# Graph attention network on one core: operands of VectorE's long instructions moved from SBUF to PSUM, and a new order of scores, messages and transposes

## What is computed

```
m = xl[src] + xr[dst]
e = einsum('ehd,hd->eh', leaky_relu(m, 0.2), att)
emax = segment_max(e, dst);  ex = exp(e - emax[dst])
denom = segment_sum(ex, dst);  alpha = ex / denom[dst]
out = segment_sum(alpha[..., None] * xl[src], dst)
```

## Time and profile before

| | us |
|---|---|
| median of 3 runs (lowest to highest) | 7290.55 (7282.23 to 7300.37) |
| span of the profiled execution | 7290.4 |
| busy in it: PE / DVE / ACT / POOL | 4733.5 / 4893.6 / 4079.6 / 5179.0 |
| share of the span: PE / DVE / ACT / POOL | 65% / 67% / 56% / 71% |
| mean granted clock of TensorE | 0.792 |

### The profile page before, as it was taken

The page is one execution under the profiler, slowest core; times in us unless marked ns, Lnnn a source line. Parts: engine busy times, 40 slices in busy tenths (PEclk is TensorE's granted clock), DMA queues, the critical chain, the costliest instruction groups (busy, mean ns, idle before and its releaser), DMA issues. The chain is left out here.

```text
span 7290.4 us, 132506 instructions
## 1 busy us (share of the span) xinstructions
PE 4733.5 (65%) x30647; PEld 4262.1 (58%) x30647; DVE 4893.6 (67%) x9144; ACT 4079.6 (56%) x9739; POOL 5179.0 (71%) x5105
## 2 busy tenths in 40 slices
PE   2777776577777567777746666645666654666663
PEld 2677775466767457777635565535555553555553
DVE  5777886467777557777655555546777765777776
ACT  1555554466766457667623333326767654767672
POOL 4777774377777577777657777757777766777774
PEclk6777787788888778888868778867888876888886
DMA  2677775289998578898847777735555553555553
GB/s 71 183 192 194 194 196 157 69 251 258 259 261 256 154 219 258 255 261 255 228 116 208 206 203 206 206 102 148 159 159 159 159 139 97 159 159 159 159 159 88
DMA packets 1717674, 1334.47 MB, mean 183 GB/s; under 512 B 384948, under 2 KB 1559891, under 8 KB 1717524
## 3 DMA queue, kind: packets, MB, share of 16 engines
q1 hardware_dynamic: 1516788, 837.31, 40.0%
q0 software_dynamic: 200736, 495.45, 24.8%
HBM read 913.26 MB, written 418.79 MB: 183 GB/s over the span
## 5 line engine op out<-in xcount | busy, mean ns | idle before, releaser
L739 POOL DMA_INDIRECT s_rows<-kv_tab,s_idx x2352 | 2359.8, 1003 | 737.3 <-issue 703.8
L739 POOL DMA_INDIRECT s_rows<-xl_tab,s_idx x1568 | 1622.5, 1035 | 491.6 <-issue 476.8
L902 PE MATMUL bank<-s_qwin,s_hot_t 128*128 128x128 f32 (+1 forms) x9408 | 1657.2, 342 | 12.9 <-ACT s_hot_t L766 7.1
L928 PE MATMUL bank<-s_msg,s_hot 128*128 128x144 f32 (+1 forms) x9408 | 1553.5, 313 | 126.1 <-ACT s_part L810 90.9
L902 PEld LDWEIGHTS bank<-s_qwin,s_hot_t 128*128 128x128 f32 x9408 | 1557.9, 256 | 57.0 <-issue 31.0
L928 PEld LDWEIGHTS bank<-s_msg,s_hot 128*128 128x128 f32 x9408 | 1351.1, 211 | 189.0 <-ACT s_part L810 145.1
L917 PE MATMUL bank<-ident,s_alpha 128*32 128x128 f32 (+1 forms) x588 | 182.6, 310 | 1512.8 <-DVE s_alpha L1042 1506.1
L810 ACT ACTIVATE s_part<-bank 128x288 f32<-128x288 f32 (+1 forms) x2352 | 901.2, 403 | 352.5 <-PE bank L928 299.7
L917 PEld LDWEIGHTS bank<-ident,s_alpha 128*32 128x32 f32 (+1 forms) x588 | 62.6, 107 | 1598.6 <-issue 1598.4
L780 ACT ACTIVATE s_gap<-iota_free,rank_col 128x128 bf16<-128x128 f32 x3136 | 989.5, 387 | 0.1
L798 ACT ACTIVATE s_prob<-s_diff 32x128 f32<-32x128 f32 (+1 forms) x588 | 180.3, 307 | 1436.2 <-DVE s_diff L997 1407.5
(11 more groups left out here) (292 smaller groups left out, 6193.9 us busy)
## 6 DMA issues: line engine op xcount, KB each, us to landing
s_qwin<-q_tab SPq DMA_DIRECT2D x3920, 64.0 KB
part_tab<-s_part SPq DMA_DIRECT2D x294, 576.0 KB
part_tab<-s_part SPq DMA_DIRECT2D x294, 544.0 KB
s_attr_t<-attr_tab SPq DMA_DIRECT2D x196, 512.0 KB
attr_tab<-s_attr_t SPq DMA_DIRECT2D x98, 512.0 KB
s_rows<-kv_tab,s_idx POOLq DMA_INDIRECT x2352
s_rows<-xl_tab,s_idx POOLq DMA_INDIRECT x1568
s_attr<-in_edge_attr SPq DMA_DIRECT2D x97, 256.0 KB
```

What stands on the lines that cost most here:

```text
L739: pool.indirect_dma_start(out=rows[u][:, t, :], out_offset=None, in_=tab, in_offset=bass.IndirectOffsetOnAxis(ap=idx[u][:, t:t + 1], axis= ...
L902: ins = pe.matmul(q_ps[h][:, (t - h * per) * QW:(t - h * per + 1) * QW], hot_t[:, t, :], qwin[u][:, t, :], start=True, stop=True)
L928: ins = pe.matmul(part_ps[c % 2][:, t * W:(t + 1) * W], hot[u][:, PAIR * c + t, :], msg[:, PAIR * c + t, :], start=True, stop=True)
```

## The change

In `edge_sweep`:

- Constants (the row 0..127 for the one-hots, Wt, bt, att) are copied once a sweep from SBUF into PSUM bank 4, and the one-hots, the angles and the product with att read them there. The angle itself is kept in bank 2, and the first scan's result `fwd` in bank 5.
- messages read probabilities and maxima from PSUM. `copy_probs` and `pm` are gone; `msg` has two buffers; turn_alpha(i) waits for messages(i-1) in place of copy_probs(i-1).
- gatv2: the add (new L1036) writes into the q bank in place, ScalarE `slopes` (new L805) multiplies the bank by 0.2 into `prod`, and VectorE `weigh` takes the maximum of bank and `prod` (new L1048), multiplies with att (new L1050) and sums (new L1051). Both adds stand before both weighs.
- gat: the one-hots are bf16 too and ScalarE casts them; the last step of the angles, -|a|, becomes `folds` on ScalarE (Abs) with a negative scale in the cosine; angles stand before the scores; turn_attr and copy_attr go half by half through one bank.
- In every sweep messages(n-1) stay behind all of scores(n) on VectorE.

```diff
-        hot_ps = [pl.banks[0], pl.banks[2]] if kind == "gat" else [pl.banks[0][:, :].bitcast(BF16)]
+        hot_ps = pl.banks[0][:, :].bitcast(BF16)
         q_ps = [pl.banks[1], pl.banks[2]]
         e_ps = [pl.banks[3], pl.banks[4]]
+        if kind == "gat":
+            ang_ps, turn_ps = pl.banks[2], pl.banks[3]
+        const = pl.banks[4]
+        iota_ps, Wt_ps, bt_ps, att_ps = const[:, 0:P], const[:, P:P + 64], const[:, P + 64:2 * P], const[:, P:2 * P]
         small = pl.banks[5]
         alpha_t = small[0:R, 0:P]
+        fwd = small[0:R, 3 * P:4 * P]
         prob_ps, max_ps = small[:, P:P + R], small[:, P + R:P + 2 * R]
         part_ps = [pl.banks[6], pl.banks[7]]
 
...
-                def copy_probs(i, k, u, n):
-                    wait(act, prob_turned, i + 1)
-                    if n >= 1:
-                        wait(act, msg_done, 3 * i)
-                    act.activation(pm[:, :], small[:, P:P + 2 * R], ACT.Copy).then_inc(prob_copied, 1)
+                def slopes(i, k, u, n):
+                    for h in range(2):
+                        wait(act, added, 2 * i + h + 1)
+                        act.activation(prod[h][:, :, :].rearrange("p t d -> p (t d)"), q_ps[h][:, :], ACT.Copy, scale=0.2
+                                       ).then_inc(slope_done, 1)
...
+                def folds(i, k, u, n):
+                    wait(act, angle_done, i + 1)
+                    act.activation(ang2[u][:, :, :], ang2[u][:, :, :], ACT.Abs).then_inc(folded, 1)
...
                     if has(n, 1):
                         copy_hot(*near(*g, 1))
+                    if kind == "gatv2" and has(n):
+                        slopes(*g)
                     if has(n, -2):
                         copy_parts(*near(*g, -2), 0)
                         copy_parts(*near(*g, -2), 1)
-                    if has(n, -1):
-                        copy_probs(*near(*g, -1))
...
                 def turn_alpha(i, k, u, n):
                     wait(pe, alpha_done, QB * (i + 1))
                     if n >= 1:
-                        wait(pe, prob_copied, i)
+                        wait(pe, msg_done, 3 * i)
                     settle(pe, pe_passed)
                     pe.transpose(alpha_t, alpha[:, :, :].rearrange("p t h -> p (t h)"), pl.ident[:, :]
                                  ).then_inc(alpha_turned, 1)
...
-                    out = hot[u] if kind == "gat" else hot_b[u % 2]
-                    v.tensor_tensor(out[:, :, :], bc(pl.iota_free[:, :].unsqueeze(1), [P, G, P]),
+                    v.tensor_tensor(hot_b[u % 2][:, :, :], bc(iota_ps.unsqueeze(1), [P, G, P]),
                                     bc(pl.rank_col[:, bass.ds(i * G, G)].unsqueeze(2), [P, G, P]),
                                     ALU.is_equal).then_inc(hot_built, 1)
...
+                def scores(i, k, u, n, h):
+                    if h == 0:
+                        wait(v, gathered[u], 16 * G * (k + 1))
+                        if n >= 1:
+                            wait(v, alpha_turned, i)
+                    wait(v, q_done, 2 * i + h + 1)
+                    t0, t1 = h * HALF, (h + 1) * HALF
+                    q = q_ps[h][:, :].rearrange("p (t d) -> p t d", t=HALF)
+                    if kind == "tconv":
+                        e = e_ps[h][:, :].rearrange("p (t d) -> p t d", t=HALF)
+                        kv = rows[u][:, t0:t1, :].rearrange("p t (a d) -> p t a d", a=2)
+                        v.tensor_tensor(kv, kv, bc(e.unsqueeze(2), [P, HALF, 2, D]), ALU.add).then_inc(e_used, 1)
+                        wait(v, e_used, 2 * i + h + 1)
+                    if kind == "gatv2":
+                        v.tensor_tensor(q, q, rows[u][:, t0:t1, :], ALU.add).then_inc(added, 1)
+                    else:
+                        v.tensor_tensor(prod[h][:, :, :], q, rows[u][:, t0:t1, 0:D], ALU.mult).then_inc(q_used, 1)
+                        wait(v, q_used, 2 * i + h + 1)
                         v.tensor_reduce(alpha[:, t0:t1, :], prod[h][:, :, :].rearrange("p t (h c) -> p t h c", c=C),
                                         AX.X, ALU.add).then_inc(alpha_done, 1)
 
+                def weigh(i, k, u, n, h):
+                    then = stepper(i, h)
+                    wait(v, slope_done, 2 * i + h + 1)
+                    t0, t1 = h * HALF, (h + 1) * HALF
+                    flat = prod[h][:, :, :].rearrange("p t d -> p (t d)")
+                    v.tensor_tensor(flat, q_ps[h][:, :], flat, ALU.max).then_inc(q_used, 1)
+                    wait(v, q_used, 2 * i + h + 1)
+                    then(v.tensor_tensor(prod[h][:, :, :], prod[h][:, :, :], bc(att_ps.unsqueeze(1), [P, HALF, D]), ALU.mult))
+                    v.tensor_reduce(alpha[:, t0:t1, :], prod[h][:, :, :].rearrange("p t (h c) -> p t h c", c=C),
+                                    AX.X, ALU.add).then_inc(alpha_done, 1)
+
                 def angles(i, k, u, n):
 
 
+                    wait(v, gathered[u], 16 * G * (k + 1))
                     then = stepper(i)
                     fl = "p t c -> p (t c)"
-                    a, tn = ang[:, :, :].rearrange(fl), turns[:, :, :].rearrange(fl)
+                    a, tn = ang_ps[:, :], turns[:, :, :].rearrange(fl)
+                    a3 = a.rearrange("p (t c) -> p t c", t=G)
                     then(v.tensor_tensor(rel[:, :], rows[u][:, :, D + H], pl.weight_col[:, bass.ds(i * G, G)], ALU.subtract))
                     then(v.tensor_tensor(ang[:, :, :], bc(rel[:, :].unsqueeze(2), [P, G, 64]),
-                                         bc(w["Wt"][:, :].unsqueeze(1), [P, G, 64]), ALU.mult))
-                    then(v.tensor_tensor(ang[:, :, :], ang[:, :, :], bc(w["bt"][:, :].unsqueeze(1), [P, G, 64]), ALU.add))
+                                         bc(Wt_ps.unsqueeze(1), [P, G, 64]), ALU.mult))
+                    then(v.tensor_tensor(a3, ang[:, :, :], bc(bt_ps.unsqueeze(1), [P, G, 64]), ALU.add))
                     then(v.tensor_scalar(tn, a, float(1 / (2 * np.pi)), MAGIC, ALU.mult, ALU.add))
                     then(v.tensor_scalar(tn, tn, MAGIC, None, ALU.subtract))
                     then(v.scalar_tensor_tensor(a, tn, -TWO_PI_HIGH, a, ALU.mult, ALU.add))
-                    then(v.scalar_tensor_tensor(a, tn, -TWO_PI_LOW, a, ALU.mult, ALU.add))
                     if n >= S:
                         wait(v, cos_done, i - S + 1)
-                    v.scalar_tensor_tensor(ang2[u][:, :, :].rearrange(fl), a, -1.0, a, ALU.mult, ALU.min
+                    v.scalar_tensor_tensor(ang2[u][:, :, :].rearrange(fl), tn, -TWO_PI_LOW, a, ALU.mult, ALU.add
                                            ).then_inc(angle_done, 1)
 
...
                 def messages(i, k, u, n):
-                    wait(v, prob_copied, i + 1)
-                    if n >= 1:
-                        wait(v, part_done, NPAIR * i)
+                    out = msg[u % 2]
+                    wait(v, prob_turned, i + 1)
+                    if n >= 2:
+                        wait(v, part_done, NPAIR * (i - 1))
                     vals = rows[u][:, :, TW - D:TW] if kind in ("tconv", "mha") else rows[u][:, :, 0:D]
-                    p = pm[:, 0:R].rearrange("p (t h) -> p t h", h=H)
-                    v.tensor_copy(msg[:, :, D:D + H], p).then_inc(msg_done, 1)
-                    v.tensor_tensor(msg[:, :, 0:D].rearrange("p t (h c) -> p t h c", c=C),
+                    p = prob_ps.rearrange("p (t h) -> p t h", h=H)
+                    v.tensor_copy(out[:, :, D:D + H], p).then_inc(msg_done, 1)
+                    v.tensor_tensor(out[:, :, 0:D].rearrange("p t (h c) -> p t h c", c=C),
                                     vals.rearrange("p t (h c) -> p t h c", c=C),
                                     bc(p.unsqueeze(3), [P, G, H, C]), ALU.mult).then_inc(msg_done, 1)
 
-                    v.tensor_tensor(msg[:, :, D + H:W], pm[:, R:2 * R].rearrange("p (t h) -> p t h", h=H),
+                    v.tensor_tensor(out[:, :, D + H:W], max_ps.rearrange("p (t h) -> p t h", h=H),
                                     bc(pl.last_col[:, bass.ds(i * G, G)].unsqueeze(2), [P, G, H]), ALU.mult
                                     ).then_inc(msg_done, 1)
 
...
+                    else:
+                        if has(n):
+                            scores(*g, 0)
+                            if kind == "gatv2":
+                                scores(*g, 1)
+                        if has(n):
+                            if kind == "gatv2":
+                                weigh(*g, 0)
+                                weigh(*g, 1)
+                            else:
+                                scores(*g, 1)
+                        if has(n, -1):
+                            messages(*near(*g, -1))
                     if not act_builds and has(n, 2):
                         build_hot(*near(*g, 2))
```

141 lines of the change are left out of this document (61 added, 80 removed).

## The result

The changed kernel takes **7369.81 us** (median of 4 runs, 7364.21 to 7371.11), the kernel before in the same comparison 7287.07 (7282.23 to 7300.37): a ratio of **1.0108**, 95% interval 1.0094 to 1.0123. It is slower by about 1.1%, more than the 0.3% that can be told from no change. Its profiled execution spans 7362.4 us (before 7290.4) at a granted clock of 0.779 (before 0.792). The prediction's range, 7000 to 7410, holds the time; its figure, 7298, is 72 us too low.

The account below looks back on a forecast made before the run. GpSimd's gathers were taken to set the pace inside every sweep. The terms -64 - 35 - 35 - 50 + 96 + 96 = +8 on 7290 us gave 7298 us, range 7000 to 7410.

Parts of the forecast that it names:

- a PSUM input frees a gather: All sweeps: gathers beginning inside a long VectorE instruction with a PSUM input aren't held; stretching to remove, 336 us together.
- Rival 4: All sweeps: a PSUM input frees nothing, gathers stay stretched and the gatv2 loop stays; 7482 us, chance 0.04.
- mha's 50: mha sweep: the whole gather stretch of 50 us is gained, since its scores are half as long.
- gat's 64: gat sweep: the whole gather stretch of 64 us is gained, since its angles are not in the turn-of-alpha loop.
- two SBUF inputs: VectorE, all sweeps: a gather begun inside a long instruction with both inputs in SBUF waits for its end.
- 35 a sweep: Each tconv sweep: 35 us of gain, near the 42 of a free loop, with turns now waiting for the messages.
- the 42%: tconv: share of groups at which a mix of 9.35 and 10.9 us loops passes GpSimd's 10.0 us.
- rival 3: tconv also closes its loop as more groups run spread at 1.2 GHz; 7460 us, about 7368 at 70%; chance 0.10.
- the largest term: Each gatv2 sweep: a closed loop of 11.7 us a group, against 10.72 before, becomes the bound and costs 96 us more.
- rival 2: gatv2: the slopes close no loop and GpSimd keeps the pace everywhere; 6954 us, chance 0.10.
- Rival 1: gatv2: the clock stays up, loop 10.2 us by maxima, exps and measure, -50 a sweep; 7006 us, chance 0.14.
- the sign on GpSimd: gatv2, at 11.4 to 12.2 us a group: gathers in packs, GpSimd's idle time between them released by the messages.

Follow-up runs that it names:

- e4: Changed kernel with ScalarE's copy of the probabilities into SBUF restored, read by the messages and awaited by turn_alpha; 7230.60 us, 0.9883 of the kernel before.
- e1: Changed kernel with spread(n+1) issued ahead of turn_alpha(n) on TensorE in all sweeps; 7108.25 us, 0.9729 of the kernel before.
- e2: Changed kernel with slopes(n) issued ahead of copy_hot(n+1) on ScalarE, gatv2 alone; 7050.52 us, 0.9654 of the kernel before.
- e11: Changed kernel with the turn of alpha in its own PSUM bank (mha, gatv2), not waiting for messages; 7056.90 us, 0.9671 of the kernel before.
- e3: Changed kernel with 12 unread identity matmuls on TensorE ahead of each turn_alpha in gatv2; 7058.27 us, 0.9660 of the kernel before.
- e5: Same kernel as e11, in a comparison with halts of ScalarE and VectorE; 10334.28 us beside 10096.87 for the kernel before, ratio 1.0232.
- e9: Same kernel as e11, run again in a comparison with halts; 10271.15 us beside 9963.12 for the kernel before, ratio 1.0322.

## Why the prediction was right, and where it was not

That the time lies between 7000 and 7410 says little by itself: the range is 410 us wide, and the figure was the difference of a gain of 184 and a loss of 192. What was right and wrong shows in the terms.

**The gathers' stretch, right.** The sentence that a PSUM input frees a gather holds: e4 gave one copy in SBUF back and with it the whole stretch of mha and tconv. The inference of the Trainium skill's page SBUF — State Buffer ("Who interferes with whom"), that a `tensor_tensor` leaves the gathers of GpSimd alone, isn't borne out: by it e4 would have changed no gather, and 50 us came back in mha. Rival 4 is out. Of the terms, mha's 50 came as 50.1 and gat's 64 as 55.3: 3.5 us of stretch are left there and 5 of gaps. Most of the 3.5 comes from an instruction that the prediction has no term for, a step of the angles whose only tensor input is in SBUF:

```profile
707.39 0.43 DVE L1067 TENSOR_SCALAR s_turns<-s_turns 128x512 f32<-128x512 f32 x1
707.45 1.18 POOL L744 DMA_INDIRECT s_rows<-gat_tab,s_idx  x1 [0.30 <-issue]
```

The gather ends 0.81 us after it, as behind the others; 15 gathers of gat do so. So "two SBUF inputs" was too narrow a rule, by 3 us. (One reading of rows 1 was off, and nothing rests on it: VectorE is busy 0.58 of mha's stretch, not 0.71 or more, and TensorE is busier than VectorE in tconv, 0.75, and in mha, 0.65.)

**tconv, right in kind, half in size.** I took 35 a sweep; 26 and 24 came up to the last gather, 21 and 17 with the end. The loop does pass 10.0 only where spread runs at the lower clock in part or whole (11.18 in the row above, where I had 10.9, and 9.25 where I had 9.35). But 61 of 97 turns did, more than the 42% at which by my own sum the loop takes over. So rival 3's mechanism came, far milder than its 7368 to 7460: the mean is 10.25, not 10.44 or 10.9.

**gatv2, right, and a little short.** The step that the largest term rested on, one closed loop through slopes, weigh, messages, turn_alpha, spread, turn_hot and copy_hot, was 11.7 us by my sum and is 11.64 in the shorter of its two turns. Step by step it is 0.92 (0.92 taken), 0.62 (0.65), 4.09 (4.12), 1.48 and 0.14 (1.60) and 4.39 (4.4). In the other turns the last step is 4.9, near the slowest of my three rows (4.92), and its mean is 4.60. The 4.4 was a choice between rows and not a sum, so part of the nearness to 11.64 is luck. 96 were taken for each sweep; 92 and 95 came up to the last gather, 104 and 106 with the end. Three cuts at three of its steps (e1, e2, e11) each brought the turns down to 10.2; rival 2 is out. Rival 1, the clock that stays up, has its place right and its condition not met: with the clock held up by added work (e3) the loop is 10.24 and goes by maxima, exps and measure, and I had 10.2. What I named as the sign on GpSimd was wrong: its gaps are ended by the copy of the indices on ScalarE (372.6 us), hardly by the messages (1.2).

**The ends of the sweeps: the step that failed.** "-64 - 35 - 35 - 50 + 96 + 96 = +8" counts sweeps and nothing between them. Up to their last gathers the sweeps made +31 (-55, -26, -24, -50, +92, +95), so the terms were 23 us too good, 20 of these in tconv and 9 in gat, less some 5 in gatv2. The other 41 us of the 72 were not in the sum at all: they lie behind five of the six sweeps, where GpSimd's lead has to be worked off. In e4, where GpSimd sets the pace again, the 41 are gone (909 between and behind, 914 before); in e2 26 of them are left. It could have been foreseen: where a producer loses its place as the bound, its queue stands full when it ends. With the 41 us the sum would have been 7339. Nor are they a cost of their own. The loop that is the bound runs for all 98 groups, the gathers end sooner, and with its end each sweep made -50, -21, -17, -50, +104 and +106. Counted so, the missing 64 us between the forecast +8 and the measured +72 are 32 in tconv, 18 in gatv2 and 14 in gat. In tconv and gatv2 the mean length of the loop was taken too short, since spread ran at the lower clock for more of the groups, or for longer, than I took. In gat the loop had no term at all: its turns are 10.20 us apart, and 10.04 in e1, where spread doesn't stand behind the turn that waits for the messages.

## What to carry to other kernels

Before giving a fast producer more speed, walk the in-order queues of all engines once round and sum the steps of each closed loop over one iteration: durations of the old trace gave 11.7 us for a loop that takes 11.64 and 12.16 in turn, 11.84 on average. Where a step has two lengths, as with TensorE's two clocks, work out how often each comes. If such a loop binds, swap two neighbours in one queue before giving the idea up: one swap on ScalarE turned 1.011 into 0.965, while one on TensorE helped one kind of sweep and hurt another. And count a stage to the end of its last group, not to the producer's last piece: the producer's lead hides a part of the slower loop, and it is paid at the end.

## What the hardware showed that I had not expected

- Every gather that VectorE holds ends 0.81 to 0.83 us after the end of the instruction that held it (1056 of the 1058 over 1.0 us in the kernel before), and how long it is held is a matter of phase: 94 gathers a sweep behind the same multiply cost 67 us in one sweep of e4 and 24 in the next.
- Matmuls whose result nobody reads make the changed kernel 4% faster (7370 to 7058): in gatv2 the granted clock goes from 0.79 to 1.00, spread from 3.59 to 2.05 us, where TensorE had idled 3.65 us before each turn.
- VectorE writes a sum in place into a PSUM bank as fast as into SBUF: L1036, of 512 elements from the bank and the rows into the bank, takes 0.700 us, the mean of 392; L1033 into SBUF took 0.686.
- A kernel that is 3.3% faster on one chip is 2.3 to 3.2% slower than that same kernel before in the comparisons with halts of ScalarE and VectorE (e11 against e5 and e9). The time of the kernel before, 7290 or 10,000 us, tells which of the two a comparison is.
